# Eight result buffers in place of four in a mixture-of-experts stage, and its middle loops written out

## What is computed

```
x = _L0_conv_ref(x, ...)                      # attention over the pixels of each image
t = t + _L1_attn_ref(_ln_t(t), ...)           # state-space layer
...
logits = flat @ router_w.T                    # flat: 8192 tokens x 128, 8 experts
topk_probs, topk_idx = jax.lax.top_k(softmax(logits), 2)
topk_probs = topk_probs / (sum(topk_probs) + 1e-09)
h = silu(flat @ w1[e].T) * (flat @ w3[e].T)   # 341 hidden units for each expert e
y = h @ w2[e].T
out = sum over the two chosen experts of gate * y
t = t + out
```

## Time and profile before

| | us |
|---|---|
| median of 3 runs | 1212.71 |
| lowest and highest of them | 1211.24, 1214.21 |
| span of the profiled execution, first to last instruction | 1181.1 |
| stage of the slots in it, first transpose to last matmul, about | 839 to 1162 |

### The profile page before, as it was taken

The page is one execution under the profiler, slowest core; times in us unless marked ns, Lnnn a source line. Parts: engine busy times, 40 slices in busy tenths (PEclk is TensorE's granted clock), DMA queues, the critical chain, the costliest instruction groups (busy, mean ns, idle before and its releaser), DMA issues.

```text
span 1181.1 us, 29643 instructions
## 1 busy us (share of the span) xinstructions
PE 1083.7 (92%) x8432; PEld 998.3 (85%) x8433; DVE 852.1 (72%) x3071; ACT 754.7 (64%) x1903; POOL 624.9 (53%) x981
## 2 busy tenths in 40 slices
PE   3889999999999999999999999867889999999993
PEld 2779888888988988988888888856789999999883
DVE  3488888988988888888898898776355644444564
ACT  1567777777767777767777777742476666666551
POOL 8122444467557566556646655743744665444442
PEclk9999999999999999999999999976799999999997
DMA  7200000001000100100100000010122222223666
GB/s 221 61 1 28 10 2 28 6 24 39 11 25 11 38 19 18 39 20 10 46 6 24 22 13 15 10 28 10 49 60 62 80 78 74 73 64 92 173 181 183
DMA packets 76439, 57.73 MB, mean 49 GB/s; under 512 B 10725, under 2 KB 70669, under 8 KB 76301
## 3 DMA queue, kind: packets, MB, share of 16 engines
q1 hardware_dynamic: 58285, 33.75, 10.5%
q0 software_dynamic: 8704, 17.97, 4.5%
q10 hardware_dynamic: 9312, 4.33, 1.3%
HBM read 32.27 MB, written 24.81 MB: 48 GB/s over the span
## 4 chain that ended last, share of the span: by engine, by line
PE 60%; DVE 11%; POOL 10%; issue 10%; ACT 3%; DMA 2%; SPq 2%; DVEq 1%; POOLq 0%; ACTq 0%
PE pc L433 7%; PE pY L588 7%; PE pX L583 6%; PE pa L483 5%; PE pb L600 3%; PE pd L600 3%; PE pY L399 3%; DVE CV L1232 2%; PE pc L437 2%; POOL rows_by_expert L991 2%; PE pX L412 2%; PE pa L444 2%; PE pX L414 2%; PE pX L413 2%; DMA GX<-rows_by_expert 2%
## 5 line engine op out<-in xcount | busy, mean ns | idle before, releaser
L1003 POOL DMA_INDIRECT results_by_choice<-YE,DIX x144 | 143.2, 995 | 147.6 <-ACT YE L786 132.5
L991 POOL DMA_INDIRECT rows_by_expert<-XA,SL x128 | 147.6, 1153 | 35.2 <-issue 35.2
L1481 DVE TENSOR_TENSOR V<-XT,pY 128x384 f32<-128x384 f32 x144 | 79.7, 554 | 116.1 <-ACT XT L777 111.5
L433 PEld LDWEIGHTS pc<-XDT,M 128*128 128x128 f32 x1024 | 128.3, 198 | 14.0 <-issue 9.5
L433 PE MATMUL pc<-XDT,M 128*128 128x64 f32 x1024 | 126.6, 279 | 6.4 <-DVE CT L1238 6.4
L1232 DVE SCALAR_TENSOR_TENSOR CV<-XBC,cw,CV 128x256 f32<-128x256 f32 x288 | 132.0, 513 | 0.0
L483 PE MATMUL pa<-V,PT 128*128 128x128 f32 x1024 | 127.3, 278 | 0.2 <-issue 0.2
L934 POOL TENSOR_TENSOR YG<-Y,SZ 128x256 f32<-128x256 f32 x64 | 46.5, 726 | 149.5 <-DVE Y L1266 135.7
L583 PE MATMUL pX<-TA,XBC 128*128 128x128 f32 (+1 forms) x864 | 121.2, 277 | 2.3 <-ACT TA L769 1.9
L588 PE MATMUL pY<-TA,XBC 128*128 128x128 f32 (+1 forms) x864 | 121.2, 277 | 1.2 <-DVE XBC L1485 1.0
L483 PEld LDWEIGHTS pa<-V,PT 128*128 128x128 f32 x1024 | 119.3, 192 | 2.7 <-issue 0.7
(11 more groups left out here) (283 smaller groups left out, 2891.6 us busy)
## 6 DMA issues: line engine op xcount, KB each, us to landing
GX<-rows_by_expert SPq DMA_DIRECT2D x144, 65.0 KB, 1.8
XT<-in_xT_dram SPq DMA_DIRECT2D x8, 512.0 KB, 4.0
X<-in_x_dram SPq DMA_DIRECT2D x16, 256.0 KB, 3.0
out_dram<-T ACTq DMA_DIRECT2D x16, 256.0 KB
results_by_choice<-YE,DIX POOLq DMA_INDIRECT x144
rows_by_expert<-XA,SL POOLq DMA_INDIRECT x128, 2.4
XA<-results_by_choice SPq DMA_DIRECT2D x8, 256.0 KB, 5.1
W<-in_w1T_dram SPq DMA_DIRECT2D x1, 1364.0 KB
```

What stands on the lines that cost most here:

```text
L433: mm(pc[:, 64 * h:64 * h + 64], M[:, h, :], XDT[:, e % 2, HD * h:HD * h + 64], start=h == 0, stop=False, skip_group_check=True)
L991: g.indirect_dma_start(xg, bass.IndirectOffsetOnAxis(ap=SL[:, j // NT, j % NT:j % NT + 1], axis=0), XA[:, j // NT, j % NT, :], None).then_ ...
L1003: g.indirect_dma_start(yg, bass.IndirectOffsetOnAxis(ap=DIX[:, j, :], axis=0), YE[:, j, :], None).then_inc(s(f"ye{j}_scattered"), 16)
L1481: tt(HT[:, par].rearrange("p k t -> p (k t)"), SH[:, par, :], pY[:, 512 * par:512 * par + HP3], ALU.mult).then_inc(s("hh_ready"), 1)
```

## The change

The buffers `YE`, `DIX` and `GATE` become eight, used in turn by slot number, each with a semaphore of its own for its scatter. `GX` stays at four. The loops over groups 14 to 24, and both loops of SP, become straight code. The core of the diff:

```
-        YE = sb("YE", [P, GROUP, C])
-        DIX = sb("DIX", [P, GROUP, 1], mybir.dt.uint32)
-        GATE = sb("GATE", [P, GROUP, 1])
+        RESULTS = 2 * GROUP
+        YE = sb("YE", [P, RESULTS, C])
+        DIX = sb("DIX", [P, RESULTS, 1], mybir.dt.uint32)
+        GATE = sb("GATE", [P, RESULTS, 1])
...
-            for g in range(LEAD):
-                group(g * GROUP)
-                between(g)
-            with eng.Fori(LEAD * GROUP, (TURN - 1) * GROUP + 1, GROUP) as t:
-                group(t)
-            for g in range(TURN, GROUPS):
+            for g in range(GROUPS):
                 group(g * GROUP)
                 between(g)
...
             def results_written(slots):
-                for j in range(GROUP):
-                    sp.wait_ge(s(f"ye{j}_scattered"), 16 // GROUP * slots)
+                for j in range(RESULTS):
+                    sp.wait_ge(s(f"ye{j}_scattered"), 16 // RESULTS * slots)
...
-            with sp.Fori(GROUP, (LEAD + 2) * GROUP + 1, GROUP) as t:
-                fetches(t)
+            for g in range(1, LEAD + 3):
+                fetches(g * GROUP)
...
-            with sp.Fori((LEAD + 7) * GROUP, TURN * GROUP + 1, GROUP) as t:
-                fetches(t)
+            for g in range(LEAD + 7, TURN + 1):
+                fetches(g * GROUP)
...
-                if not (isinstance(t, int) and t == 0):
-                    act.wait_ge(s(f"ye{j}_scattered"), t * 4)
-                A(YE[:, j, :], (pd, pb)[j % 2][:, 0:C], ACT.Copy, scale=GATE[:, j, 0:1]).then_inc(s("ye_ready"), 1)
+                y = (t + j) % RESULTS
+                if n > RESULTS:
+                    act.wait_ge(s(f"ye{y}_scattered"), 16 * ((n - 1) // RESULTS))
+                A(YE[:, y, :], (pd, pb)[j % 2][:, 0:C], ACT.Copy, scale=GATE[:, y, 0:1]).then_inc(s("ye_ready"), 1)
...
-                if not (isinstance(t, int) and t == 0):
-                    dve.wait_ge(s(f"ye{j}_scattered"), t * 4)
-                v.tensor_copy(DIX[:, j, :], GX[:, j, C + 1:C + 2])
-                v.tensor_copy(GATE[:, j, :], GX[:, j, C:C + 1]).then_inc(s("dix_ready"), 1)
+                y = (t + j) % RESULTS
+                if t + j >= RESULTS:
+                    dve.wait_ge(s(f"ye{y}_scattered"), 16 * ((t + j) // RESULTS))
+                v.tensor_copy(DIX[:, y, :], GX[:, j, C + 1:C + 2])
+                v.tensor_copy(GATE[:, y, :], GX[:, j, C:C + 1]).then_inc(s("dix_ready"), 1)
```

More of the change, by code:

```diff
@@ L318, in fetch @@
                 row = sp.value_load(TBI[0:1, 0, bass.ds(t + j, 1)], min_val=0, max_val=ROWS - P)
-                if not (isinstance(t, int) and t == 0):
+                if not (t == 0):
                     sp.wait_ge(s("gxt_ps"), t + j + 1 - GROUP)
@@ L592, in result @@
                 pe.wait_ge(s("hh_ready"), n)
-                if not isinstance(n, int) or n > 2:
+                if n > 2:
                     pe.wait_ge(s("ye_ready"), n - 2)
@@ L607, in between @@
                     def between():
-                        if not (isinstance(t, int) and t + j == SLOTS - 1):
+                        if not (t + j == SLOTS - 1):
                             x_T(t, j + 1)
                     hidden(t + j + 1, j % 2, between)
-                    if not (isinstance(t, int) and t + j == 0):
+                    if not (t + j == 0):
                         result(t + j, (j - 1) % 2, experts[j])
@@ L796, in group @@
                         gate(t, j - 2)
-                    elif not (isinstance(t, int) and t == 0):
+                    elif not (t == 0):
                         gate(t - GROUP, GROUP + j - 2)
@@ L1002, in put @@
                 apart(pool)
-                g.indirect_dma_start(yg, bass.IndirectOffsetOnAxis(ap=DIX[:, j, :], axis=0), YE[:, j, :], None).then_inc(s(f"ye{j}_scattered"), 16)
+                y = (t + j) % RESULTS
+                g.indirect_dma_start(yg, bass.IndirectOffsetOnAxis(ap=DIX[:, y, :], axis=0), YE[:, y, :], None).then_inc(s(f"ye{y}_scattered"), 16)
             def group(t):
@@ L1501, in group @@
                     take_gates(t, j)
-                    if isinstance(t, int) and t // GROUP in ADDS:
+                    if t // GROUP in ADDS:
                         add(ADDS[t // GROUP], j)
-                    if isinstance(t, int) and t + j in TABLE:
+                    if t + j in TABLE:
                         (table_counts, table_firsts, table_slots, table_tiles, table_experts, table_digits)[TABLE[t + j]](1)
```

## The result

Faster by half a per cent, outside the range: the median of the changed kernel is 1204.85 us (1202.04 to 1214.29, 20 runs), that of the kernel before 1211.03 us (1208.60 to 1214.21, 20 runs), the ratio 0.995 (0.9939 to 0.9961).

What follows compares the result with a forecast made beforehand. TensorE (PE), busy 92% of the span, was taken to bound the kernel; 0.35 us from buffers, 0.17 from loops and 0 from instruction blocks took 1212.71 to 1212.2 us, with an 8-in-10 range of 1208.6 to 1215.0.

Steps and rivals of the forecast that it cites:

- the sum: Whole kernel: 0.35 + 0.17 + 0 = 0.52 us less, from 1212.71 to 1212.2 us, with 31.6 us around the span unchanged.
- the part on the loops: Loops written out: PE gains 0.17 us over groups 14 to 24; SP's, POOL's and DVE's gaps lie beside full PE.
- the term of the loops: PE's loop over groups 14 to 24: writing it out gains 0.17 us, bounds 0 and 0.17 on PE.
- Eight buffers, first groups: Slots 4 to 7 no longer wait for a scatter; slots 6 and 7 stand 2.11 us apart, gaining 0.35 us.
- Eight buffers, the end: Last groups: DVE's scatter waits, up to 1.97 us, are slack; removing them gains 0, and PE's 5.0 us of holes stay.
- the chain of waits: Last groups: one turn of 10.30 us runs through PE, DVE, SP's loads and the slow fetch, with no scatter in it.
- The rival of recovering fetches: Last groups: earlier indices free earlier fetches, PE's 5.0 us of holes go, giving 1207.2 us; chance 0.15.
- that of colliding ones: Last groups: fetches freed sooner collide with SP's loads, costing PE 6.84 us, giving 1219.0 us; chance 0.11.
- PE's back edges: Groups 14 to 24: back edge, register sums and register waits cost PE 0.17 us in all, gained when written out.
- The rival of ACT's 0.40 us gap: ACT's gap before each loop iteration's first weight copy, eleven times, on the path: 4.4 us gained, 1208.3 us; chance 0.03.
- Instruction blocks: Middle groups written out: about six more blocks on PE's instruction queue, cost 0; rival up to 17.9 us slower, chance 0.03.

Runs made afterwards that it cites:

- c1: The kernel before, unchanged, run and profiled again: 1212.17 us, ratio 1.0006; its profiled execution took 1215.53 us, span 1213.7.
- e1: The kernel before with all loops written out and four buffers kept: 1206.65 us, ratio 0.9962 to the kernel before.
- e2: The changed kernel with eight buffers but the loops kept, middle loop taking two groups an iteration: 1215.27 us, ratio 1.0024 to the kernel before.
- e12: Four buffers, loops written out on PE, ACT, DVE and POOL, SP's two loops kept: ratio to the kernel before not below 1 beyond its interval.
- e16: The kernel before with SP's two loops alone written out, second time, on one chip with all loops written out: ratio 0.9964.
- e15: The kernel before with all loops written out, four buffers, second time, on one chip with SP's loops alone written out: ratio 0.9927.
- e6: The changed kernel with late routed-row scatters set apart, behind a group's second and fourth result scatters: 1208.41 us, ratio 0.9947 to the kernel before.
- e5: The kernel before with late routed-row scatters set apart, behind a group's second and fourth result scatters: 1207.72 us, ratio 0.9951.
- e9: The changed kernel with late routed-row scatters in four runs of four instead of eight pairs: 1212.54 us, ratio 1.0004 to the kernel before.
- e8: The kernel before with late routed-row scatters in four runs of four instead of eight pairs: 1212.37 us, ratio 1.0017.
- after: The changed kernel's first profile: profiled execution 1202.8 us, span 1201.1 us.
- c2: The changed kernel, unchanged, run again for a second trace: 1205.92 us, ratio 0.9959 to the kernel before.
- e7: The changed kernel with added copies nobody reads: POOL scatters behind groups 15, 17, 19, 23, plain ACT-queue copies behind 25; 1217.0 us in one execution.

## Why the prediction was wrong, step by step

**The step that failed** is in the sum: "The median of the runs shown is 1212.71, 31.6 us above that span (launch and end, which the change leaves alone)". Around a span lie 1.7 to 1.9 us in every run (c1 1215.53 and 1213.7). The other 30 us were inside ordinary executions and missing from the one profiled: for the most part holes in groups 7 to 15 (some 27 us more there in c1), where the prediction saw a full PE. From that followed the second error, in the part on the loops: "SP's, POOL's and DVE's gaps lie beside a full PE". In ordinary executions PE idles 9.0 of 47.4 us in groups 12 to 15 (c1). So the term of the loops, 0.17 us, was mis-sized: the loops written out alone took 5.2 us off (e1, 1206.65 beside 1211.9). The 31.6 us did no harm as a number, since the sum started from the median of the runs; what they hid is the idle time of PE that made this term too small.

**Eight buffers, first groups**, 0.35 us: not there. e2 shows no gain, and in these groups the holes cover it (slots 5, 6 and 7 of the changed kernel's timeline begin 5.1 and 4.2 us apart, not 2.11).

**Eight buffers, the end**, 0: right. DVE's waits went, PE's wait for fetched rows stayed (4.5 us), as the chain of waits had said. The rival of recovering fetches and that of colliding ones both fall.

**PE's back edges**, 0.17 us: right in size for PE. Groups 16 to 20 take 8.44 to 8.51 us in the loop and 8.44 written out. The rival of ACT's 0.40 us gap (its 1208.3 is counted from 1212.7, where the other rivals start at 1212.2) forecast a gain of the right size for a wrong reason: eleven such gaps would show as 4.4 us in groups 14 to 24, but groups 16 to 27, nine of the eleven among them, take 102.72 us with the loops (c1) and 102.23 without.

**Instruction blocks**, six more at no cost: right in number for the queue that was counted (72 and 66), and no cost is seen: groups 16 to 20 take 8.44 us each in straight code.

**Where the gain is**, shown: in the loops (e1, e2), not without SP's (e12), about half of it by SP's alone where both were run on one chip (e16 beside e15); and it can no longer be told where the late rows do not stand in pairs (e6 beside e5, e9 beside e8). Over profiled executions with pairs, groups 12 to 15 take 46.4 to 48.2 us with SP's loops kept (five) and 39.2 to 44.0 with all loops written out (after, c2, e1, e7, e15), means 47.0 and 41.4: 5.7 us. The same executions differ elsewhere too: groups 7 to 11 take 58.3 and 54.8 us in the mean, and the slots begin at 841.0 and 837.8. So the gain is not shown to lie in groups 12 to 15 alone.

**Open.** How SP's loop lengthens holes: SP issues a fetch 0.2 us (median) after DVE's copy of the gate in either form, and PE waits for no fetch there. Why the first profiled execution had no late signals. Its trace holds 14,742 semaphore records, the nineteen others 11,822 to 12,168: the one execution without late signals is also the one with the most records. Of the 2,688 that c1 has fewer, 2,183 are of landings of DMAs, and they are missing ahead of the slots too (1,395 in place of 1,975 from 200 to 830 us), where none of PE's recorded signals is over 0.2 us late. The recording itself remains a rival as the cause of the late signals. The Trainium skill ("NOTIFIC — the notification-queue block", section 7.1) says that the block which writes such records holds back its producers rather than lose a record inside; no run here shows whether that delays PE's signals, as all runs were recorded. Whether the slots begin earlier because of the change: no instruction differs ahead of them, and they began at 837.3 to 839.9 us in eight executions with all loops written out, at 837.2 to 843.6 in the twelve others.

## What to carry to other kernels

Compare a profile's span with the times of the runs first: a gap of 31.6 us is no launch until a second profile says so, and "hidden beside a full engine" holds only for executions in which it is full. Scatters issued from POOL without a pause held up what other engines hear from PE in nineteen of the twenty profiled executions, so order them with that in mind. An edit's gain may come from shifting work against such a disturbance, and then it goes when the disturbance is ordered otherwise (0.9947 beside 0.9951).

## What was not expected of the hardware

In e7, runs of three to five scatters of 128 rows, 1.26 us apart on POOL, held back PE's signals to ACT and DVE by as much as 1.9 us (one more scatter of 512 bytes a row), 2.4 (one of 520), 3.5 (two of 520) and 4.2 (two of 512), while two plain copies from ACT's queue did not. Each time four of the held signals then came together within 0.2 us, 0.8 to 1.1 us after the last scatter of the run had ended on POOL (the first at 1094.32, where that one ended at 1093.55). ACT's and DVE's signals to PE were not late.

The disturbance can also feed itself, with no scatters but those of results. In e15, POOL stood still for 2.75 us in group 21 and then issued three without a pause; from then on the results of two slots came ready together, and their scatters went out in pairs 1.41 us apart:

```profile
1058.13 0.96 POOL L998 DMA_INDIRECT results_by_choice<-YE,DIX  x1 [2.51 <-ACT YE L781]
1059.54 0.96 POOL L998 DMA_INDIRECT results_by_choice<-YE,DIX  x1 [0.45 <-issue]
```

With each pair PE's signals are recorded 1.0 to 1.1 us late, and groups 21 to 27 take 9.0 to 9.1 us in place of 8.44.

Such a hole can cost twice. Windows around one in the kernel before (c1):

```profile
989.00:996.00 7.00, 5.01 (x46) 4.78 (x44) 1.29 (x7) 2.74 (x9) 4.78 (x5) 1.00 0.20 58
996.00:1003.00 7.00, 5.52 (x26) 5.53 (x27) 2.77 (x12) 2.58 (x8) 1.60 (x2) 0.52 0.14 40
1003.00:1010.00 7.00, 5.92 (x52) 5.73 (x52) 1.60 (x7) 2.67 (x9) 3.32 (x5) 1.00 0.21 57
```

PE had been idle for 2.0 of the seven us ahead; in the next seven its granted clock is 0.52, the lower of the two levels (1.2 GHz in place of 2.4) for nearly all of them, and 26 matmuls keep it busy for 5.52 us where 46 had taken 5.01. In groups 12 to 15 PE's busy time rose from 33.84 to 38.41 us for the same work, at a granted clock of 1.00 and 0.93. Not all of that is the clock's: the changed kernel has 35.68 us there at 1.00, and its holes there (3.5 us) did not lower the clock.
